# One quantising chain over 1536 values a step in the FFN tail of a graph transformer layer

## The chip, the cores and the metric

The kernel runs on one core of a Trainium2 chip. Its time is the device time of an execution in microseconds; the time shown for a kernel is the median of its runs. The engines meant below are TensorE (PE), VectorE (DVE), ScalarE (ACT), GpSimd (POOL) and SyncE (SP), each with its own queue of instructions that run in order and wait for semaphores.

## The reference

The layer adds to `x` (1250 rows of 1024) a graph attention over 40000 edges and a linear (softmax-free) attention, and then a feed-forward block whose three products run on values rounded to FP4 (NVFP4: 16 values share one FP8 scale). The feed-forward part, which the change touches:

```
def fake_quant_nvfp4(x, global_scale):
    xb = x.reshape(sh[:-1] + (sh[-1] // BLOCK, BLOCK))            # BLOCK = 16
    amax = jnp.max(jnp.abs(xb), axis=-1, keepdims=True)
    sc8 = jnp.clip(amax / FP4_MAX * global_scale, 0.0, FP8_MAX).astype(jnp.float8_e4m3fn)
    dq = sc8 / global_scale
    a = jnp.clip(jnp.abs(xb) / safe_dq, 0.0, FP4_MAX)
    q = jnp.sign(xb) * _FP4_VALS[jnp.digitize(a, _FP4_MIDS)]
    return (q * dq).reshape(sh)
gate_out = nvfp4_linear(x, gate_w, s_in[0])                      # x: layernormed rows, 1024 wide
up_out = nvfp4_linear(x, up_w, s_in[0])
hidden = jax.nn.silu(gate_out) * up_out                          # 512 wide
return nvfp4_linear(hidden, down_w, s_in_down[0])
```

## The kernel before

The 1250 rows are held as C = 10 chunks of 128. Most of the kernel (to about 720 us) gathers messages for the graph attention on GpSimd, VectorE and ScalarE while TensorE works through large fp32 products. The tail, from about 720 us to the end, is a software pipeline over the chunks, written out by hand for each engine as a loop over steps k. It is in these lines:

- VectorE (L1658 to L1674), step k: residual additions that are due (`residual`, L1592: PSUM product plus the stored row, with its sum); `tail_scales(k)`, which forms the gated product of chunk k-1 (L1558), the block maxima of its 512 values and of the 1024 normalised values of chunk k+1 (L1247), and from both together the FP8 scales and their inverses (`scales`, L1212 to L1222); `rows_rounded(k+1)`, the chain of eight instructions of `quantized` (L1236 to L1244) over the 1024 values, which ends with `q_done`; residuals due at (k, 1); `hidden_rounded(k-1)`, the same chain over the 512 values, which ends with `h_done`; residuals due at (k, 2). Every instruction of a chain waits for the one before through a semaphore (`step`), except the last.
- TensorE, step k: `turn_q(k+1)` (L922, transposes of the quantised rows, waits for `q_done`); x2 products due (L900 and L903, fp32; for chunks 6 to 9 and a half of 5 they include 16 products, a residual's bank must be free); `down(k-2)` (transposes L944, products L955); `gate_up(k+1)` (L933).
- ScalarE, step k: `turn_over(k+1)` (L1153, copies the transposed rows, `q_taken`); `normalize(k+2)` (L1018, L1019, `ln2_done`); the copy of the transposed products of chunk k-2 (L1180); silu of chunk k+1 (L1188) behind `gate_up(k+1)`; `scale_down(k-2)` (L1145); `deviation` of a chunk whose residuals are complete (L1130 to L1135), at places fixed by the plan.
- GpSimd takes the root for a deviation (L712) and adds the scaled products of a chunk to the stored output (L718); SyncE stores rows.

Which x2 product is made and added at which step is fixed in the table `X2_PLAN` (chunk, half, bank, made at, added at): (8,1) and (8,0) are made in steps 2 and 3, (9,1) in step 4 in the bank of (8,0), (9,0) in step 5 in the same bank. (8,0) is added at (4, 1), (9,1) at (5, 1) and (9,0) at (6, 1), which in the kernel before is between the two chains of a step. Products for chunks 0 to 9 of the feed-forward block run with steps -1 to 12.

`ln2` (normalised rows), `silu` and `hidden` are separate pieces of the memory `round_mem`; `ln2` and `silu` are doubled by parity, `hidden` is single.

Of the kernel before, what the change touches and what calls it, by code (L numbers as in the profile page):

```python
# [6 lines left out]
ALU = mybir.AluOpType  # L7
# [3 lines left out]
BF16 = mybir.dt.bfloat16  # L11
I32 = mybir.dt.int32
U8 = mybir.dt.uint8
U16 = mybir.dt.uint16
# [4 lines left out]
D = 1024  # L19
# [7 lines left out]
I = 512  # L27
C = 10
EARLY = 6
NC = 128  # L30
# [3 lines left out]
KB = D // P  # L34
# [14 lines left out]
FP4_MAX, FP8_MAX = 6.0, 448.0  # L49
QB = 16  # L50
SCALE = (D // 16) ** -0.5
EXPONENT = 0x7F800000
CELL, MIDDLE = 0xFFE0, 0x0010
BINADE, HALF_BIT = 0x7F80, 0x0040
# [62 lines left out]
def gps_layer(nc, x, src, dst, rms_w, w_down, wl, wr, att, w_up, wq, bq, wk_t, bk, wv_t, bv,  # L117
# [9 lines left out]
    with ExitStack() as ctx:  # L127
# [76 lines left out]
        cscale = sb("cscale", [P, 3])  # L204
# [10 lines left out]
        acc = ps("acc", [P, 4, HALF])  # L215
# [52 lines left out]
        tail_scaled = sem("tail_scaled")  # L268
# [11 lines left out]
        q_done, q_tp, q_taken = sem("q_done"), sem("q_tp"), sem("q_taken")  # L280
        gu_full, silu_done, hid_done = sem("gu_full"), sem("silu_done"), sem("hid_done")
        h_done, h_tp, h_taken = sem("h_done"), sem("h_tp"), sem("h_taken")
# [4 lines left out]
        bias_bc = base[:, C - 1, :]  # L287

        tail_mem = round_mem
        silu = [tail_mem[0:NC, i * I:(i + 1) * I] for i in range(2)]  # L290
        ln2 = [tail_mem[0:NC, (1 + i) * D:(2 + i) * D] for i in range(2)]
        qa = tail_mem[0:NC, 3 * D:4 * D]
        row_cells, row_steps = (qa[:, i * I:(i + 1) * I].bitcast(BF16) for i in range(2))
        hidden = tail_mem[0:NC, 4 * D:4 * D + I]
        q_bf = [tail_mem[0:NC, (9 + i) * I:(10 + i) * I].bitcast(BF16) for i in range(2)]
        q_t = [tail_mem[:, (11 + i) * I:(12 + i) * I].bitcast(BF16).rearrange("p (k n) -> p k n", k=KB) for i in range(2)]
        h_bf = [tail_mem[0:NC, 13 * I + i * 256:13 * I + (i + 1) * 256].bitcast(BF16) for i in range(2)]
        h_t = [tail_mem[:, 14 * I + i * 256:14 * I + (i + 1) * 256].bitcast(BF16).rearrange("p (k n) -> p k n", k=4)
               for i in range(2)]
        base_at = [xhat_t[:, :, c * NC:(c + 1) * NC] for c in range(C)]  # L300
        gnn_tr = xr_sb[:, :, :].rearrange("p c f -> p (c f)")[:, 0:2 * NP].rearrange("p (k n) -> p k n", k=2)

        NB = (D + I) // QB
        blocks_of = tail_mem[0:NC, 15 * I:15 * I + 8 * NB].rearrange("p (a b) -> p a b", a=8)
        squares = tail_mem[0:NC, 15 * I + 8 * NB:16 * I + 8 * NB].bitcast(BF16)
        tail_max, tail_g = blocks_of[:, 0], blocks_of[:, 1]
# [671 lines left out]
        begun, n = ROUND_0_AT, index_of["p", 0]  # L978
        for g, (_, _, slots, _, _) in enumerate(ROUNDS):
            while n < len(groups):  # L980
                kind, i, engine = groups[n]
# [23 lines left out]
        def _(act):  # L1005
# [164 lines left out]
            for k in range(-1, C + 2):  # L1170
                if 0 <= k + 1 < C:
                    turn_over(k + 1)
                if 2 <= k + 2 < C:
                    normalize(k + 2)
                c = k - 2
                if 0 <= c < C:
                    act.wait_ge(h_tp, c + 1)
                    if c >= 2:
                        act.wait_ge(down_full, c - 1)
                    nc.scalar.copy(h_t[c % 2][:, :, 0:NC], tpb[:, 1, 0:4 * P].rearrange("p (k n) -> p k n", k=4)[:, :, 0:NC]).then_inc(h_taken, 1)  # L1180
                for c in whole_at((k, 0)) if k >= 0 else []:
                    deviation(c)
                c = k + 1
                if 0 <= c < C:
                    act.wait_ge(gu_full, c + 1)
                    if c >= 2:
                        act.wait_ge(hid_done, c - 1)
                    nc.scalar.activation(silu[c % 2], acc[0:NC, 2, :], ACT.Silu, scale=cscale[0:NC, 0:1]).then_inc(silu_done, 1)  # L1188
                if 0 <= k - 2 < C - 1:
                    scale_down(k - 2)  # L1190
                for c in [*whole_at((k, 1)), *whole_at((k, 2))] if k >= 0 else []:
                    deviation(c)

        @block.vector
        def _(dve):
            steps = [0]

            def step(ins):

                steps[0] += 1  # L1200
                ins.then_inc(dve_step, 1)
                dve.wait_ge(dve_step, steps[0])
# [21 lines left out]
            def quantized(v, to, factors, cell, way, width):  # L1224


                sc8, inv = factors
                nb = width // QB
                rows_in = v.shape[1] // width

                def turned_blocks(a):
                    return a.rearrange("p (r i b) -> p r i b", r=rows_in, i=QB)

                high = v.bitcast(U16).rearrange("p (r b i t) -> p r i b t", r=rows_in, i=QB, t=2)[:, :, :, :, 1]
                by_block = v.rearrange("p (b i) -> p b i", i=QB)
                step(nc.vector.tensor_tensor(by_block, by_block, inv.unsqueeze(2).to_broadcast([v.shape[0], rows_in * nb, QB]), ALU.mult))  # L1236
                step(nc.vector.tensor_scalar(turned_blocks(cell.bitcast(U16)), high, CELL, MIDDLE, ALU.bitwise_and, ALU.bitwise_or))
                step(nc.vector.tensor_scalar(way.bitcast(U16), cell.bitcast(U16), BINADE, HALF_BIT, ALU.bitwise_and, ALU.bitwise_or))
                step(nc.vector.tensor_scalar(way, way, 1.5, 64.0, ALU.max, ALU.mult))
                step(nc.vector.tensor_tensor(cell, cell, way, ALU.add))  # L1240
                step(nc.vector.tensor_tensor(way, cell, way, ALU.subtract))
                step(nc.vector.tensor_scalar(way, way, -FP4_MAX, FP4_MAX, ALU.max, ALU.min))
                spread = sc8.rearrange("p (r b) -> p r b", r=rows_in).unsqueeze(2).to_broadcast([v.shape[0], rows_in, QB, nb])
                return nc.vector.tensor_tensor(turned_blocks(to), turned_blocks(way), spread, ALU.mult)  # L1244

            def block_max(to, v):
                return nc.vector.tensor_reduce(to, v.rearrange("p (b i) -> p b i", i=QB), AX.X, ALU.max,  # L1247
                                               apply_absolute_value=True)
# [299 lines left out]
            def tail_scales(k):  # L1548


                lo, hi = 0 if k + 1 < C else D // QB, NB if k - 1 >= 0 else D // QB
                if k == -1:
                    nc.vector.tensor_copy(tail_g[:, 0:D // QB], s_in_bc[0:NC, 0:1].to_broadcast([NC, D // QB]))
                    step(nc.vector.tensor_copy(tail_g[:, D // QB:], s_in_bc[0:NC, 1:2].to_broadcast([NC, I // QB])))
                if k - 1 >= 0:
                    c = k - 1
                    dve.wait_ge(silu_done, c + 1)
                    nc.vector.scalar_tensor_tensor(hidden, acc[0:NC, 3, :], cscale[0:NC, 1:2], silu[c % 2], ALU.mult, ALU.mult).then_inc(hid_done, 1)  # L1558
                    dve.wait_ge(hid_done, c + 1)
                    ins = block_max(tail_max[:, D // QB:], hidden)  # L1560
                if k + 1 < C:
                    dve.wait_ge(ln2_done, k + 2)
                    ins = block_max(tail_max[:, 0:D // QB], ln2[(k + 1) % 2])
                step(ins)
                sc8, inv = tail_factors[k % 2]
                scales(tail_max[:, lo:hi], tail_g[:, lo:hi], (sc8[:, lo:hi], inv[:, lo:hi]),
                       (blocks_of[:, 2, lo:hi], blocks_of[:, 3, lo:hi])).then_inc(tail_scaled, 1)

            def rows_rounded(c):
                dve.wait_ge(tail_scaled, c + 1)  # L1570
                if c >= 2:
                    dve.wait_ge(q_tp, c - 1)
                sc8, inv = tail_factors[(c - 1) % 2]
                quantized(ln2[c % 2], q_bf[c % 2], (sc8[:, 0:D // QB], inv[:, 0:D // QB]), row_cells, row_steps, D).then_inc(q_done, 1)

            def hidden_rounded(c):
                dve.wait_ge(tail_scaled, c + 3)
                if c >= 2:
                    dve.wait_ge(h_tp, c - 1)
                sc8, inv = tail_factors[(c + 1) % 2]  # L1580
                quantized(hidden, h_bf[c % 2], (sc8[:, D // QB:], inv[:, D // QB:]), row_cells[:, 0:I], row_steps[:, 0:I], I).then_inc(h_done, 1)

            def residual(c, h):

# [75 lines left out]
            for k in range(-1, C + 3):  # L1660
                for i in added_at((k, 0)):
                    residual(*i)
                if k <= C:
                    tail_scales(k)
                if 0 <= k + 1 < C:
                    rows_rounded(k + 1)
                for i in added_at((k, 1)):
                    residual(*i)
                if k - 3 == C - 1:
                    finish(k - 3)  # L1670
                if 0 <= k - 1 < C:
                    hidden_rounded(k - 1)
                for i in added_at((k, 2)):
                    residual(*i)  # L1674

# [24 lines left out]
```

## Time and profile before

| | |
|---|---|
| median of 3 runs | 917.87 us (916.38 to 919.6) |
| profiled execution | 920.16 us |
| its span | 918.4 us |
| PE busy | 856.0 us (93%) |
| DVE busy | 817.6 us (89%) |
| ACT busy | 549.5 us (60%) |
| POOL busy | 498.9 us (54%) |
| mean granted clock of TensorE | 0.968 |

The span is the time from the first to the last instruction of the profiled execution; what lies around it makes its own time. All positions below are microseconds from the span's start. In a timeline, the busy time of an instruction is printed behind its start; where an instruction does not wait for the one ahead of it, it can start before that one's printed end. A chain "of 1024" is one whose instructions work on 1024 values in each of 128 partitions.

### The profile page before, as it was taken

How to read it: one execution, taken by the hardware profiler on the slowest of the kernel's cores; microseconds unless marked ns; L12 is line 12 of the kernel's file. 1: busy time of each engine (PE TensorE's matmuls, PEld its weight loads, DVE VectorE, ACT ScalarE, POOL GpSimd, SP SyncE). 2: the span in 40 equal slices, each digit the busy share in tenths (PEclk: the TensorE clock that was granted, in tenths of full speed). 3: DMA queues.
4: the chain of work that ended last, by engine and by line, in shares of the span. 5: the costliest groups of instructions: out<-in, count | busy, mean ns of one | idle time of the engine just before them, and what ended most of it. 6: DMA issues, size and time to landing. Idle time of an engine off the chain costs nothing.

```text
span 918.4 us, 9530 instructions
## 1 busy us (share of the span) xinstructions
PE 856.0 (93%) x2734; PEld 417.5 (45%) x2734; DVE 817.6 (89%) x987; ACT 549.5 (60%) x1947; POOL 498.9 (54%) x528
## 2 busy tenths in 40 slices
PE   4999999999999999999999999997999699999665
PEld 3885455644444444444444444432444244444222
DVE  7989988779999999999999999999994277999994
ACT  3313123356767887779898988798995332353432
POOL 5200748578667777777777787877775200010011
PEclk9999999999999999999999999997999899999877
DMA  9322625563655333663345633349959911113125
GB/s 306 98 95 52 179 85 178 143 196 99 84 162 184 97 89 89 193 202 107 102 122 172 193 97 100 91 111 190 382 111 204 207 49 46 69 24 69 24 46 87
DMA packets 72403, 117.85 MB, mean 128 GB/s; under 512 B 29383, under 2 KB 42340, under 8 KB 72330
## 3 DMA queue, kind: packets, MB, share of 16 engines
q0 software_dynamic: 27520, 63.68, 30.2%
q1 hardware_dynamic: 44826, 53.52, 18.6%
q8 instruction: 22, 0.36, 0.2%
q14 instruction: 35, 0.29, 0.1%
HBM read 89.15 MB, written 17.17 MB: 116 GB/s over the span
## 4 chain that ended last, share of the span: by engine, by line
DVE 61%; PE 14%; issue 9%; POOL 8%; DMA 6%; ACT 1%; ACTq 0%; SPq 0%; POOLq 0%; DVEq 0%
DVE acc_sb L1487 12%; DVE turned L1479 11%; DVE z L1639 11%; DVE turned L1637 10%; PE acc L745 3%; POOL round_mem L550 3%; PE turned L900 2%; DMA round_mem<-msg_table,idx 2%; PE acc L933 2%; DMA acc_sb<-gnn_dram 2%; PE acc L900 2%; PE turned L955 1%; POOL round_mem L628 1%; POOL perm_dram L599 1%; POOL xr_sb L632 1%
## 5 line engine op out<-in xcount | busy, mean ns | idle before, releaser
L550 POOL DMA_INDIRECT round_mem<-msg_table,idx x352 | 345.5, 982 | 99.5 <-issue 80.0
L1122 ACT ACTIVATE round_mem<-round_mem,pz 128x65 f32<-128x65 f32 x1408 | 354.1, 398 | 7.0 <-DVE acc_sb L1487 3.0
L745 PE MATMUL acc<-wslot,big_a 128*128 128x512 f32 x512 | 220.3, 592 | 0.0
L745 PEld LDWEIGHTS acc<-wslot,big_a 128*128 128x128 f32 x512 | 97.1, 190 | 121.5 <-issue 121.3
L1487 DVE TENSOR_REDUCE acc_sb<-round_mem 128x260 f32<-128x1820 f32 (+1 forms) x62 | 121.6, 1962 | 7.2 <-ACT round_mem L1122 5.1
L1479 DVE TENSOR_TENSOR turned<-round_mem,turned 128x1560 f32<-128x1560 f32 (+1 forms) x62 | 105.4, 1700 | 7.4 <-DMA round_mem<-msg_table,idx 5.4
L1112 ACT ACTIVATE pz<-z 128x7 f32<-128x7 f32 (+1 forms) x248 | 55.4, 296 | 93.7 <-DVE z L1644 93.6
L745 PE MATMUL acc<-big_b,wslot 128*128 128x512 f32 x256 | 110.1, 592 | 0.2 <-ACT big_b L1058 0.2
L745 PE MATMUL acc<-wslot,big_b 128*128 128x512 f32 x256 | 110.0, 592 | 0.0
L1639 DVE TENSOR_REDUCE z<-turned 128x24 f32<-128x1560 f32 (+1 forms) x62 | 105.1, 1695 | 2.1
L1637 DVE SCALAR_TENSOR_TENSOR turned<-turned,att_sb 128x1536 f32<-128x1536 f32 (+1 forms) x62 | 103.6, 1671 | 0.0
L745 PE MATMUL acc<-big_a,xhat_t 128*128 128x512 f32 x192 | 84.8, 605 | 6.8 <-ACT big_a L1065 6.8
L745 PE MATMUL acc<-big_b 128*128 128x512 f32 (+3 forms) x240 | 80.6, 495 | 0.0
L745 PEld LDWEIGHTS acc<-big_b,wslot 128*128 128x128 f32 x256 | 48.6, 190 | 61.7 <-issue 60.5
L745 PEld LDWEIGHTS acc<-wslot,big_b 128*128 128x128 f32 x256 | 48.6, 190 | 61.2 <-issue 60.7
L712 POOL TENSOR_TENSOR rstd<-small,minus_half 128x1 f32<-128x1 f32 x10 | 6.3, 632 | 107.0 <-ACT small L1135 107.0
L745 PEld LDWEIGHTS acc<-big_a,xhat_t 128*128 128x128 f32 x192 | 37.2, 194 | 54.4 <-issue 46.8
L745 PEld LDWEIGHTS acc<-big_b 128*128 128x128 f32 x240 | 43.1, 194 | 35.3 <-issue 29.6
L667 POOL TENSOR_TENSOR round_mem<-acc_sb,pz 128x260 f32<-128x260 f32 x62 | 45.6, 736 | 21.8 <-DVE acc_sb L1487 21.0
L718 POOL DMA_DIRECT2D out_x<-acc_sb x9 | 8.0, 892 | 72.7 <-ACT acc_sb L1145 72.7
L1188 ACT ACTIVATE round_mem<-acc,cscale 128x512 f32<-128x512 f32 x10 | 6.9, 688 | 62.5 <-PE acc L933 62.5
L1055 ACT COPY big_a<-acc 128x512 f32<-128x512 f32 x16 | 9.2, 587 | 58.1 <-PE acc L745 42.6
(231 smaller groups left out, 1045.4 us busy)
## 6 DMA issues: line engine op xcount, KB each, us to landing
round_mem<-msg_table,idx POOLq DMA_INDIRECT x352, 2.8
big_b<-in_x SPq DMA_DIRECT2D x9, 512.0 KB, 7.7
big_b<-big_b SPq DMA_DIRECT2D x9, 512.0 KB, 13.2
big_b<-in_x POOLq DMA_DIRECT2D x9, 512.0 KB, 12.8
out_x<-big_b SPq DMA_DIRECT2D x9, 512.0 KB, 3.2
out_x<-acc_sb POOLq DMA_DIRECT2D x9, 512.0 KB, 5.4
wslot<-in_wv_t SPq DMA_DIRECT2D x2, 2048.0 KB, 9.3
wslot<-in_wk_t SPq DMA_DIRECT2D x2, 2048.0 KB, 9.5
```

The source lines that it names most:

```text
L550: pool.indirect_dma_start(xg[g % 4][:, j, :], None, msg_table, bass.IndirectOffsetOnAxis(idx[:, c, j0 + j:j0 + j + 1], 0)).then_inc(xg_in[ ...
L667: nc.gpsimd.tensor_tensor(halves_of[g % 3][:, :, :, n].rearrange("p i (h d) -> p i h d", d=MR), running[c].rearrange("p (i h d) -> p i h d ...
L745: mm = nc.tensor.matmul(o(acc[:, n % 4, :]), a, b, start=first, stop=last)
L900: nc.tensor.matmul(to, xhat_t[:, k, c * NC:(c + 1) * NC], mat_a[:, k, h * HALF:(h + 1) * HALF], start=(k == 0), stop=False)
L933: mm = nc.tensor.matmul(acc[0:NC, 2 + h, :], q_t[c % 2][:, k, 0:NC], wgu_sb[:, k, h * HALF:(h + 1) * HALF], start=(k == 0), stop=(k == KB ...
L1055: nc.scalar.copy(mat_a[:, m, h * HALF:(h + 1) * HALF], a).then_inc(t, 1)
L1112: ins = nc.scalar.activation(pz[:, g % 2, 0:slots + 1, h], z[:, g % 3, 0:slots + 1, h], ACT.Exp, scale=-1.0, bias=z[:, (g + 1) % 3, top_sl ...
L1122: ins = nc.scalar.activation(to[:, :, j], xg[g % 4][:, j, h * HR + 1:(h + 1) * HR], ACT.Copy, scale=pz[:, g % 2, j, h:h + 1])
L1479: return nc.vector.tensor_tensor(m4[:, 0:n], xg[g % 4][:, 0:n, :].rearrange("p j (h d) -> p j h d", d=HR)[:, :, :, 0:MR], receiver.unsquee ...
L1487: nc.vector.tensor_reduce(running[c].rearrange("p (i f) -> p i f", i=2), halves_of[g % 3][:, :, :, 0:n + 1], AX.X, ALU.add).then_inc(sum_d ...
L1637: step(nc.vector.scalar_tensor_tensor(m4[:, 0:slots, :, 1:MR], m4[:, 0:slots, :, 1:MR], 0.0, att_sb[0:NC].unsqueeze(1).to_broadcast([NC, s ...
L1639: step(nc.vector.tensor_reduce(zz[:, 0:slots, :], m4[:, 0:slots], AX.X, ALU.add))
```

## The change

The two chains of a step become one. The normalised rows of chunk k+1 and the gated products of chunk k-1 have the same parity, and stand side by side in a slab of 1536 values, two slabs by parity; the gated product is written over silu in place. One reduction takes the block maxima of both, and one chain of seven instructions runs over the 1536 values (1024 in steps -1 and 0, 512 in steps 9 and 10); its eighth, the multiplication by the scales, remains two instructions, first the one for the rows (`q_done`), then the one for the products (`h_done`). They read a part of each group of 96 block columns. Residuals that were due between the two chains come behind the fused one. ScalarE's silu waits for `h_done` in place of `hid_done`. The scratch pieces move within `round_mem`.

```diff
-        silu = [tail_mem[0:NC, i * I:(i + 1) * I] for i in range(2)]
-        ln2 = [tail_mem[0:NC, (1 + i) * D:(2 + i) * D] for i in range(2)]
...
-        hidden = tail_mem[0:NC, 4 * D:4 * D + I]
+        NB = (D + I) // QB
+        slab = [tail_mem[0:NC, i * (D + I):(i + 1) * (D + I)] for i in range(2)]
+        ln2, silu = [a[:, 0:D] for a in slab], [a[:, D:D + I] for a in slab]
+        row_cells, row_steps = (tail_mem[0:NC, 6 * I + 768 * i:6 * I + 768 * (i + 1)].bitcast(BF16) for i in range(2))
...
                     if c >= 2:
-                        act.wait_ge(hid_done, c - 1)
+                        act.wait_ge(h_done, c - 1)
...
-                    nc.vector.scalar_tensor_tensor(hidden, acc[0:NC, 3, :], cscale[0:NC, 1:2], silu[c % 2], ALU.mult, ALU.mult).then_inc(hid_done, 1)
+                    nc.vector.scalar_tensor_tensor(silu[c % 2], acc[0:NC, 3, :], cscale[0:NC, 1:2], silu[c % 2], ALU.mult, ALU.mult).then_inc(hid_done, 1)
                     dve.wait_ge(hid_done, c + 1)
-                    ins = block_max(tail_max[:, D // QB:], hidden)
                 if k + 1 < C:
                     dve.wait_ge(ln2_done, k + 2)
-                    ins = block_max(tail_max[:, 0:D // QB], ln2[(k + 1) % 2])
-                step(ins)
+                step(block_max(tail_max[:, lo:hi], slab[(k + 1) % 2][:, lo * QB:hi * QB]))
...
-            def rows_rounded(c):
...
-            def hidden_rounded(c):
...
+            def step_rounded(k):
+                lo, hi = 0 if k + 1 < C else D // QB, NB if k - 1 >= 0 else D // QB
+                n = hi - lo
+                dve.wait_ge(tail_scaled, k + 2)
+                if k >= 1 and k + 1 < C:
+                    dve.wait_ge(q_tp, k)
+                if k >= 3:
+                    dve.wait_ge(h_tp, k - 2)
+                sc8, inv = (f[:, lo:hi] for f in tail_factors[k % 2])
+                v = slab[(k + 1) % 2][:, lo * QB:hi * QB]
+                by_block = v.rearrange("p (b i) -> p b i", i=QB)
+                high = v.bitcast(U16).rearrange("p (b i t) -> p i b t", i=QB, t=2)[:, :, :, 1]
+                cell, way = row_cells[:, 0:n * QB], row_steps[:, 0:n * QB]
+                step(nc.vector.tensor_tensor(by_block, by_block, inv.unsqueeze(2).to_broadcast([NC, n, QB]), ALU.mult))
...
+                step(nc.vector.tensor_scalar(way, way, -FP4_MAX, FP4_MAX, ALU.max, ALU.min))
+                way = way.rearrange("p (i b) -> p i b", i=QB)
+                for there, to, b0, b1, done in ((k + 1 < C, q_bf, 0, D // QB, q_done), (k - 1 >= 0, h_bf, D // QB, NB, h_done)):
+                    if there:
+                        nc.vector.tensor_tensor(to[(k + 1) % 2].rearrange("p (i b) -> p i b", i=QB), way[:, :, b0 - lo:b1 - lo],
+                                                sc8[:, b0 - lo:b1 - lo].unsqueeze(1).to_broadcast([NC, QB, b1 - b0]), ALU.mult).then_inc(done, 1)
...
-                if 0 <= k + 1 < C:
-                    rows_rounded(k + 1)
+                if k <= C:
+                    step_rounded(k)
                 for i in added_at((k, 1)):
                     residual(*i)
...
-                if 0 <= k - 1 < C:
-                    hidden_rounded(k - 1)
```

## Rows read from the trace of the kernel before

**Rows 1.** Windows, 840 to 860: stretch, length, busy PE/PEld/DVE/ACT/POOL, PEclk, DMA share, GB/s
```profile
840.00:860.00 20.00, 17.24 (x75) 7.91 (x73) 18.93 (x40) 8.74 (x14) 1.54 (x3) 1.00 0.18 28
```

**Rows 2.** Timeline, VectorE, step 4: start, us, engine line op, shapes [idle before <-releaser]
```profile
815.67 1.22 DVE L1247 TENSOR_REDUCE round_mem<-round_mem 128x64 f32<-128x1024 f32 x1 [0.96 <-ACT round_mem L1019]
```

**Rows 3.** Timeline, VectorE, step 2: gated product, maxima, scales, start of the rows' chain
```profile
780.57 0.75 DVE L1558 SCALAR_TENSOR_TENSOR round_mem<-acc,cscale,round_mem 128x512 f32<-128x512 f32 x1
781.36 0.69 DVE L1247 TENSOR_REDUCE round_mem<-round_mem 128x32 f32<-128x512 f32 x1
782.91 1.22 DVE L1247 TENSOR_REDUCE round_mem<-round_mem 128x64 f32<-128x1024 f32 x1 [0.87 <-ACT round_mem L1019]
784.17 0.26 DVE L1212 SCALAR_TENSOR_TENSOR round_mem<-round_mem 128x96 f32<-128x96 f32 x1
...
787.11 1.23 DVE L1236 TENSOR_TENSOR round_mem<-round_mem 128x1024 f32<-128x1024 f32 x1
```

**Rows 4.** Timeline, all engines, step 7: from the rows' multiply to the next maxima
```profile
872.44 0.69 DVE L1244 TENSOR_TENSOR round_mem<-round_mem 128x1024 bf16<-128x1024 bf16 x1
...
873.18 0.62 PE L922 MATMUL turned<-identb,round_mem 128*128 128x128 bf16 x8 [3.02 <-DVE round_mem L1244]
...
873.84 1.01 ACT L1153 COPY round_mem<-turned 128x1024 bf16<-128x1024 bf16 x1
...
875.14 1.24 ACT L1019 ACTIVATE round_mem<-big_b,less_mean,rstd 128x1024 f32<-128x1024 f32 x1
...
877.41 0.69 DVE L1247 TENSOR_REDUCE round_mem<-round_mem 128x32 f32<-128x512 f32 x1
```

**Rows 5.** Timeline, VectorE: last multiplies of step 2's two chains, and of step 8's rows
```profile
792.27 0.69 DVE L1244 TENSOR_TENSOR round_mem<-round_mem 128x1024 bf16<-128x1024 bf16 x1
792.88 0.69 DVE L1236 TENSOR_TENSOR round_mem<-round_mem 128x512 f32<-128x512 f32 x1
...
796.13 0.42 DVE L1244 TENSOR_TENSOR round_mem<-round_mem 128x512 bf16<-128x512 bf16 x1
796.47 0.69 DVE L1592 SCALAR_TENSOR_TENSOR big_b<-acc,big_b 128x512 f32<-128x512 f32 x1
...
887.35 0.69 DVE L1244 TENSOR_TENSOR round_mem<-round_mem 128x1024 bf16<-128x1024 bf16 x1
```

**Rows 6.** Timeline, ScalarE: the copies L1153 of chunks 3 and 4, and what precedes
```profile
796.83 0.99 ACT L1153 COPY round_mem<-turned 128x1024 bf16<-128x1024 bf16 x1
...
809.55 0.69 ACT L1188 ACTIVATE round_mem<-acc,cscale 128x512 f32<-128x512 f32 x1 [3.42 <-PE acc L933]
810.14 1.11 ACT L1145 ACTIVATE acc_sb<-turned,cscale 128x1024 f32<-128x1024 f32 x1
...
813.18 0.99 ACT L1153 COPY round_mem<-turned 128x1024 bf16<-128x1024 bf16 x1
```

**Rows 7.** Timeline, TensorE, from the turning of q(3) to that of q(5)
```profile
794.01 0.61 PE L922 MATMUL turned<-identb,round_mem 128*128 128x128 bf16 x8
...
809.78 0.62 PE L922 MATMUL turned<-identb,round_mem 128*128 128x128 bf16 x8 [0.26 <-DVE round_mem L1244]
...
821.68 3.62 PE L933 MATMUL acc<-wslot,round_mem 128*128 128x512 bf16 x16
825.78 0.62 PE L922 MATMUL turned<-identb,round_mem 128*128 128x128 bf16 x8 [0.49 <-DVE round_mem L1244]
```

**Rows 8.** Timeline, VectorE: the last residual, with the feed-forward result of chunk 9
```profile
911.61 1.28 DVE L1597 SCALAR_TENSOR_TENSOR big_b<-turned,cscale,big_b 128x1024 f32<-128x1024 f32 x1 [5.45 <-PE turned L955]
```

**Rows 9.** Timeline, TensorE: down(1), and down(4) with gate_up(7) behind it
```profile
819.94 1.90 PE L955 MATMUL turned<-wslot,round_mem 128*128 128x512 bf16 x8 [0.68 <-ACT round_mem L1180]
...
862.40 3.59 PE L955 MATMUL turned<-wslot,round_mem 128*128 128x512 bf16 x8 [3.92 <-ACT round_mem L1180]
865.79 4.37 PE L933 MATMUL acc<-wslot,round_mem 128*128 128x512 bf16 x16
```

**Rows 10.** Windows, 862 to 864 (columns as in Rows 1)
```profile
862.00:864.00 2.00, 1.60 (x4) 0.58 (x5) 1.97 (x3) 0.35 (x1) 0.00 (x0) 0.50 0.97 180
```

More of the change, by code:

```diff
@@ L289, in gps_layer @@
         tail_mem = round_mem
-        silu = [tail_mem[0:NC, i * I:(i + 1) * I] for i in range(2)]
-        ln2 = [tail_mem[0:NC, (1 + i) * D:(2 + i) * D] for i in range(2)]
-        qa = tail_mem[0:NC, 3 * D:4 * D]
-        row_cells, row_steps = (qa[:, i * I:(i + 1) * I].bitcast(BF16) for i in range(2))
-        hidden = tail_mem[0:NC, 4 * D:4 * D + I]
+        NB = (D + I) // QB
+        slab = [tail_mem[0:NC, i * (D + I):(i + 1) * (D + I)] for i in range(2)]
+        ln2, silu = [a[:, 0:D] for a in slab], [a[:, D:D + I] for a in slab]
+        row_cells, row_steps = (tail_mem[0:NC, 6 * I + 768 * i:6 * I + 768 * (i + 1)].bitcast(BF16) for i in range(2))
         q_bf = [tail_mem[0:NC, (9 + i) * I:(10 + i) * I].bitcast(BF16) for i in range(2)]
-        q_t = [tail_mem[:, (11 + i) * I:(12 + i) * I].bitcast(BF16).rearrange("p (k n) -> p k n", k=KB) for i in range(2)]
-        h_bf = [tail_mem[0:NC, 13 * I + i * 256:13 * I + (i + 1) * 256].bitcast(BF16) for i in range(2)]
+        h_bf = [tail_mem[0:NC, 11 * I + i * 256:11 * I + (i + 1) * 256].bitcast(BF16) for i in range(2)]
+        q_t = [tail_mem[:, (12 + i) * I:(13 + i) * I].bitcast(BF16).rearrange("p (k n) -> p k n", k=KB) for i in range(2)]
         h_t = [tail_mem[:, 14 * I + i * 256:14 * I + (i + 1) * 256].bitcast(BF16).rearrange("p (k n) -> p k n", k=4)
@@ L301, in gps_layer @@
         gnn_tr = xr_sb[:, :, :].rearrange("p c f -> p (c f)")[:, 0:2 * NP].rearrange("p (k n) -> p k n", k=2)
-        NB = (D + I) // QB
         blocks_of = tail_mem[0:NC, 15 * I:15 * I + 8 * NB].rearrange("p (a b) -> p a b", a=8)
@@ L1567, in tail_scales @@
                        (blocks_of[:, 2, lo:hi], blocks_of[:, 3, lo:hi])).then_inc(tail_scaled, 1)
-            def rows_rounded(c):
[L1570 to L1574, printed above, removed]
-            def hidden_rounded(c):
[L1577 to L1581, printed above, removed]
+            def step_rounded(k):
[12 more added lines that the diff above has]
+                step(nc.vector.tensor_tensor(by_block, by_block, inv.unsqueeze(2).to_broadcast([NC, n, QB]), ALU.mult))
+                step(nc.vector.tensor_scalar(cell.bitcast(U16).rearrange("p (i b) -> p i b", i=QB), high, CELL, MIDDLE, ALU.bitwise_and, ALU.bitwise_or))
+                step(nc.vector.tensor_scalar(way.bitcast(U16), cell.bitcast(U16), BINADE, HALF_BIT, ALU.bitwise_and, ALU.bitwise_or))
+                step(nc.vector.tensor_scalar(way, way, 1.5, 64.0, ALU.max, ALU.mult))
+                step(nc.vector.tensor_tensor(cell, cell, way, ALU.add))
+                step(nc.vector.tensor_tensor(way, cell, way, ALU.subtract))
+                step(nc.vector.tensor_scalar(way, way, -FP4_MAX, FP4_MAX, ALU.max, ALU.min))
[4 more added lines that the diff above has]
+                                                sc8[:, b0 - lo:b1 - lo].unsqueeze(1).to_broadcast([NC, QB, b1 - b0]), ALU.mult).then_inc(done, 1)
```

## Prediction

> **What bounds the kernel now.** Only the FFN tail is touched, so I read the busy time of each engine by stretch first. In 840 to 860 us VectorE is busy 18.93 us of 20 and TensorE 17.24 [rows 1]: two engines close to full, so a saving on one is soon stopped by the other, and by whoever hands work between them. Then the timeline of VectorE: its last idle time before the end of the loop is 0.96 us ahead of the block maxima at 815.67, for the normalised rows from ScalarE [rows 2]; from there to the last multiply of step 8 at 887.35 it runs without a gap. Ahead of that, step 2 begins after TensorE's x2 product (its maxima wait 0.87 us for ScalarE too) [rows 3]. Last, the handover. Quantised rows q(k+1) leave VectorE; TensorE turns them; ScalarE copies them (L1153) and only behind that copy, in its own order, normalises chunk k+2 (L1018, L1019), which VectorE needs for the block maxima of step k+1. In step 7 this path reads: L1244 of 1024 values starts at 872.44 and ends at 873.13, the turning starts 873.18, the copy 873.84, L1019 875.14, ending 876.38 [rows 4]. That is 3.25 us from q done to the next normalised rows, 3.3 with the start of their user. Today VectorE works through the 512-value chain of the gated products meanwhile, and asks for the rows only with the second maxima instruction, about 878.0 (the first starts at 877.41 [rows 4] and takes 0.59 more when not waited for), so 1.6 us to spare.
>
> **The change, part by part.** Steps k = 1 to 8 have both halves; steps -1, 0 (rows only), 9 and 10 (products only) keep their work.
>
> (a) Seven elementwise instructions over 1536 replace seven of 1024 and seven of 512. Seven of 1024 take 792.27 - 787.11 = 5.16 us, seven of 512 take 796.13 - 792.88 = 3.25 [rows 3, 5]. On a straight line, 512 values cost 1.91 and the fixed part of seven is 1.34; the fused seven cost 5.16 + 1.91 = 7.07. The eighth stays two instructions: q's 0.61 (792.88 - 792.27), the products' 0.34 (796.47 - 796.13). Two chains were 9.36 us, the fused one is 8.02: 1.34 less VectorE time per step, 10.7 in eight steps.
>
> (b) One TENSOR_REDUCE over 1536 for two. 512 values take 0.69, 1024 take 1.26 start to start (784.17 - 782.91) [rows 3]; on the line 1536 take 1.83. The pair took 0.59 + 1.26 when nothing was waited for, so nothing is gained (0.02). But the 512-value maxima no longer run while VectorE waits for the normalised rows: in step 2 the maxima end 0.57 later.
>
> (c) q is done later in the chain. Before, it was done 5.16 + 0.69 = 5.85 us after the chain's start; now 7.07 + 0.69 = 7.76, 1.9 later. The products are done at 8.10 in place of 9.4 to 10.0; nobody is late for them now (they are turned a step later).
>
> (d) What VectorE has to do between q done and the next need of the normalised rows shrinks from 0.5 + 3.6 + 0.75 + 0.6 to the products' multiply (0.34, about 0.25 of it behind q's end), L1558 (0.78), and a residual or two (0.61 each) in steps 4 to 6. ScalarE's 3.3 us are then no longer covered: VectorE waits some 2 us in each step. That wait replaces the saving. Behind it on VectorE stand the maxima, the scales and the whole chain, and for its q TensorE and ScalarE.
>
> (e) silu(c) waits for h_done(c-2) instead of hid_done(c-2). It is signalled 0.35 us behind q_done(c), long before gate_up(c) can end: nothing; with that cover gone it would be 0.35 us. The writing of the products over silu's buffer and the new places in memory change no size: nothing (at most a fraction of L1558's 0.75 us [rows 3], either way, and in step order it would show in that row).
>
> (f) The last multiply now reads 64 of 96 columns per group. No row shows that pattern. Lower end: 0.69 as before. Upper end: the rate of the fp32 L1236, 1.26 against 0.69; 0.57 a step, eight times 4.6. I take the lower, because its second operand is read repeated already at the same speed. In the Trainium skill, VectorE: DVE Perf Modes, What auto-detection actually checks, the fast two-operand mode wants 16-bit tensors with step 1; the pattern keeps both, and by it (f) is zero.
>
> **The sum.** Follow q_done, since everything else hangs on it. The loop without other delay: 3.3 to normalised rows, 1.83 maxima, 2.94 scales (787.11 - 784.17 [rows 3]), 7.76 chain, less the rounding of both ends, 15.75 us per step.
> Start: step 2 still begins with TensorE's product, at L1558 780.57, and its maxima at 782.91 as the rows come. q_done(3) = 782.91 + 1.83 + 2.94 + 7.76 = 795.4; before it was 792.27 + 0.69 = 792.96. Shift +2.5.
> Then six loops to q_done(9), 94.5 us, plus what ScalarE adds, where it isn't free when q has been turned (0.70 after q_done):
> - q(3): turned at 796.1, but ScalarE is in a deviation until 796.83 [rows 6], not moved by the change: +0.7.
> - q(4): silu(3), scale_down(0) and a deviation (809.55 to 813.18 [rows 6]) stand ahead of the copy and hang on gate_up(3), which moves with the turning of q(3), from 794.01 to 795.5 [rows 7]: the copy at 814.65, while q(4) = 795.4 + 15.75 + 0.7 = 811.85 is turned at 812.55: +2.1.
> - q(6): TensorE needs 15.5 us from turning one q to being ready for the next (809.78 to 821.68 + 3.62 [rows 7]). q(5) = 829.7. x2 (9,1) waits for the residual of (8,0), which now stands behind the whole chain: +0.55. gate_up(5) ends about 845.7, silu and scale_down 1.8 later (0.2 + 0.59 + 1.0): 847.5, against q(6) = 845.4 turned at 846.2: +1.3.
> - q(5), q(7), q(8): ScalarE is free or within 0.1.
> q_done(9) = 795.4 + 94.5 + 4.1 = 894.0. Before, 887.35 + 0.69 = 888.04 [rows 5]. **+6.0 us.**
> From q_done(9) to the end nothing on the path changes: its turning, gate_up(9), silu(9), the last chains of 512, down and the last residual at 911.61, which VectorE awaits for 5.45 us [rows 8]. So the end moves by the same 6.0. The profiled execution took 920.16 with a span of 918.4 (1.76 around it): span 924.4, execution 926.2. The median shown, 917.87, is 2.3 below that execution; the same 6.0 on it gives **923.9**.
>
> **Rivals.**
> (1) The fixed cost comes back; faster. If VectorE is the bound in itself, four steps (4 to 7) give 1.34 each, 5.4, and step 3 another 1.3 if TensorE's gaps of 0.26 and 0.49 [rows 7] can close; q(9) inside step 8 comes 1.9 later; end 888.0 - 6.7 + 1.9, or -4.8: 913.1. For it: VectorE has no gap after 815.67. Against: it needs the normalised rows within 1.1 us of q done, and rows 4 show 3.3. It would hold only if ScalarE normalised before copying, which its order forbids. The Trainium skill, VectorE: DVE Perf Modes, The TRN2 errata, says an operation from SBUF pays a fixed extra latency per instruction and advises bigger tiles; the trace agrees that the part exists (1.34 for seven). By that rule alone this rival would be right.
> (2) A tie. ScalarE's three delays (4.1) don't add, for they close while TensorE and VectorE wait, and residuals fit the waiting: 2.5 + 6 x 15.75, less the 95.1 that the six take now (888.04 - 792.96), is +1.9: 919.8. For it: three of six loops are undisturbed. Against: each delay was placed by a row.
> (3) TensorE's clock falls earlier; slower still. Now it is at 1.00 in 840 to 860 [rows 1] and drops to 0.50 (1.2 GHz) in 862 to 864 [rows 10], behind 3.92 us without work; the eight products there took 3.59 in place of 1.90 and the sixteen behind them 4.37 in place of 3.62 [rows 7, 9], 2.4 more together. The forecast gives gaps of 1 to 2.4 us ahead of q(4), q(5) and q(7). If one in the x2 part (the widest is ahead of q(5), 827.3 to 829.7) lowers it, and it comes back as there, that is 2.4 more: 926.3, twice 928.7. Against: gaps of 2 us stand in no full-clock part before 857, so the trace hardly says.
> (4) It doesn't do what it says, because the strided multiply is slow (f): q later by 0.57 in six loops and in step 2, 4.0 more: 927.9.
>
> **How the numbers follow.** Forecast +6.0 (4 to 7.5): 0.66. Rival 1: 0.10. Rival 2: 0.12. Rival 3: 0.08. Rival 4: 0.04. Time 923.9. Range: down to 920.5, which leaves out rival 1 and most of rival 2; up to 927.5, which takes in one fall of the clock. A measurement here can tell about 0.3%, 2.8 us. Faster 0.10, same 0.14 (rival 2 and the weakest form of the forecast), slower 0.76.
>
> **What would show it.** Right: VectorE busy some 11 us less in the tail, with an idle time of about 2 us ahead of L1247 in steps 3 to 8, ended by ScalarE's L1019; seven instructions of 1536 values whose sum is 7.07; TensorE waiting for L1244's successor 1 to 2.4 us ahead of q(4), q(5), q(7) and over 4 us ahead of q(8), q(9); the end 30.4 us behind q_done(9). Wrong: no wait ahead of L1247 (rival 1); the q multiply over 1 us (rival 4); x2 products of 512 columns at twice their time (rival 3); intervals between the q's below 15.7.

## The result and the profile after

The changed kernel takes 930.15 us (median of 4 runs, 928.43 to 931.02) against 918.15 us for the kernel before (median of 4 runs, with one more than in the table ahead of the prediction): ratio 1.0135, 95% interval 1.0114 to 1.0157. It is 12.0 us slower. The prediction said slower by 6.0, 923.9 us, range 920.5 to 927.5: the sign was right, half of the loss was missing, and the time lies outside the range. Its profiled execution took 930.23 us, with a span of 928.5.

The line of busy time of the changed kernel's page, then VectorE's table of waits from 755 us on: who waited, for whom, us in total, times, longest.

```profile
PE 857.4 (92%) x2724; PEld 417.7 (45%) x2734; DVE 807.3 (87%) x923; ACT 549.8 (59%) x1947; POOL 499.8 (54%) x528
```

```profile
DVE round_mem L1245 <- ACT round_mem L1017: 13.5, 8, 3.4
DVE round_mem L1580 <- PE turned L942: 9.5, 4, 3.9
DVE big_b L1602 <- PE acc L901: 5.5, 1, 5.5
DVE round_mem L1556 <- ACT round_mem L1186: 3.4, 1, 3.4
```

VectorE does 10.3 us less work than before (807.3 against 817.6), as the change intends. But where the table of before, from 755 us on, had 1.8 us of waits for the normalised rows, there are now 13.5, and a second wait of 9.5 us that the prediction doesn't name: the first instruction of the fused chain (L1580) waits for TensorE's turning of gated products (L942). TensorE signals this turning with the semaphore `h_tp`; VectorE may write a chunk's quantised products into their buffer only when those of two chunks earlier have been turned out of it. `q_tp` does the same for the rows. The chain itself, in the changed kernel's VectorE timeline of step 1 (answers rows 3 and rows 5 of before):

```profile
764.57 1.76 DVE L1580 TENSOR_TENSOR round_mem<-round_mem 128x1536 f32<-128x1536 f32 x1
766.37 1.46 DVE L1581 TENSOR_SCALAR round_mem<-round_mem 128x1536 uint16<-128x1536 uint16 x1
767.86 0.56 DVE L1582 TENSOR_SCALAR round_mem<-round_mem 128x1536 uint16<-128x1536 uint16 x1
...
771.04 0.56 DVE L1586 TENSOR_SCALAR round_mem<-round_mem 128x1536 bf16<-128x1536 bf16 x1
771.63 1.03 DVE L1590 TENSOR_TENSOR round_mem<-round_mem 128x1024 bf16<-128x1024 bf16 x2
772.58 0.68 DVE L1602 SCALAR_TENSOR_TENSOR big_b<-acc,big_b 128x512 f32<-128x512 f32 x1
```

Seven instructions of 1536 take 771.63 - 764.57 = 7.06 us, the two multiplies 0.95. (The row `x2` joins the multiplies of the rows and of the products.) That is the time of the two multiplies before, 0.61 and 0.34: the strided reads cost nothing.

The two waits of step 4, in the same timeline: first for the normalised rows, then, with the scales done at 820.74, for the turned products.

```profile
816.05 1.75 DVE L1245 TENSOR_REDUCE round_mem<-round_mem 128x96 f32<-128x1536 f32 x1 [3.36 <-ACT round_mem L1017]
...
820.48 0.26 DVE L1220 SCALAR_TENSOR_TENSOR round_mem<-round_mem 128x96 f32<-128x96 f32 x1
823.07 1.76 DVE L1580 TENSOR_TENSOR round_mem<-round_mem 128x1536 f32<-128x1536 f32 x1 [2.33 <-PE turned L942]
```

TensorE's timeline of the changed kernel around the same time (answers rows 7): it idles 1.92 us ahead of the turning of q(4) and of q(5), and the sixteen x2 products behind the first gap take 8.78 us, those behind the second 7.13. The second fence is the window 812 to 816, within the 8.78 us: the granted clock, 0.57 (the figure ahead of the DMA share 0.70), is mostly at its lower level of 1.2 GHz. Behind the second gap, from 831 to 835, it is 1.00.

```profile
811.75 0.62 PE L920 MATMUL turned<-identb,round_mem 128*128 128x128 bf16 x8 [1.92 <-DVE round_mem L1590]
812.21 8.78 PE L898 MATMUL acc<-big_a,xhat_t 128*128 128x512 f32 x16
820.82 1.88 PE L901 MATMUL acc<-wslot,xr_sb 128*128 128x512 f32 x4
822.54 0.39 PE L942 MATMUL turned<-identb,round_mem 128*128 128x128 bf16 x4
...
830.88 0.62 PE L920 MATMUL turned<-identb,round_mem 128*128 128x128 bf16 x8 [1.92 <-DVE round_mem L1590]
831.82 7.13 PE L898 MATMUL acc<-big_a,xhat_t 128*128 128x512 f32 x16 [0.32 <-DVE big_b L1602]
```

```profile
812.00:816.00 4.00, 4.00 (x12) 1.80 (x10) 0.69 (x2) 3.87 (x6) 1.44 (x2) 0.57 0.70 98
```

The tail of every profiled kernel can be laid out as three stretches: from the gated product of step 1 to q(3) done, from q(3) to q(9) done, and the last leg from there to the end of the span. The middle one is six loops, those of steps 3 to 8; the experiments e1 to e10 follow below. A q is done 0.69 us after its multiply starts; in the kernel before that is L1244 with 1024 values, in the changed one L1590.

| kernel | to q(3) | six loops, q(3) to q(9) | last leg |
|---|---|---|---|
| before | 32.84 | 16.76 16.00 16.29 15.57 15.55 14.91 = 95.08 | 30.36 |
| before, again (e8) | 32.84 | 16.77 15.97 16.15 15.71 15.54 14.92 = 95.06 | 28.87 |
| changed | 35.35 | 17.43 19.13 17.96 19.65 15.78 16.22 = 106.17 | 28.07 |
| forecast | 35.3 | 16.45 17.85 15.75 17.05 15.75 15.75 = 98.6 | 30.4 |
| e1 | 35.33 | 16.43 17.83 15.77 17.04 15.75 16.18 = 99.00 | 30.10 |
| e2 | 33.72 | 17.89 16.34 16.69 15.33 16.53 15.49 = 98.27 | 29.02 |
| e3 | 33.72 | 17.88 19.13 17.96 19.65 14.12 13.90 = 102.64 | 27.34 |
| e4 | 32.83 | 16.77 15.99 16.29 15.74 15.53 14.91 = 95.23 | 27.00 |
| e5 | 35.33 | 17.42 17.43 17.96 17.97 15.76 16.18 = 102.72 | 26.52 |
| e6 | 33.72 | 15.34 15.15 14.73 15.39 15.34 13.50 = 89.45 | 28.06 |
| e7 | 31.86 | 16.76 14.92 16.17 15.58 15.53 14.93 = 93.89 | 26.55 |
| e9 | 33.71 | 17.55 19.13 17.97 19.66 14.11 13.50 = 101.92 | 27.36 |
| e10 (e6 again) | 33.72 | 15.33 15.15 14.73 15.39 15.34 13.50 = 89.44 | 28.09 |

Up to q(9) the changed kernel is 2.5 + 11.1 = 13.6 us longer than before. Its last leg happens to be 2.3 shorter and it reached the tail 1.2 earlier (758.91 against 760.12): 10.1, the difference of the spans. The kernel before's profiled execution lies 2.0 above its median, which makes the 12.0 of the medians.

### The profile page after: what moved, and what is told of

It is laid out like the page before. It is cut to its first block, busy times and chain, and to the rows that moved or that the text cites. A ratio compares the mean times of both kernels' runs of the same rounds, so it can differ in the third digit from the quotient of the medians.

```text
span 928.5 us, 9458 instructions
## 1 busy us (share of the span) xinstructions
PE 857.4 (92%) x2724; PEld 417.7 (45%) x2734; DVE 807.3 (87%) x923; ACT 549.8 (59%) x1947; POOL 499.8 (54%) x528
## 4 chain that ended last, share of the span: by engine, by line
DVE 59%; PE 16%; POOL 10%; issue 10%; DMA 3%; ACT 1%; ACTq 0%; POOLq 0%; DVEq 0%
DVE acc_sb L1485 11%; DVE z L1649 10%; DVE turned L1477 10%; DVE turned L1647 10%; POOL round_mem L548 4%; PE acc L898 4%; PE acc L743 3%; PE acc L901 2%; PE turned L898 2%; DVE round_mem L1580 1%; POOL round_mem L626 1%; POOL perm_dram L597 1%; POOL xr_sb L630 1%; DVE z L1654 1%; DVE big_b L1442 1%
```

## The experiments

Three theories follow from the table of waits. Theory A: the loss that was not forecast is the wait for `h_tp` in front of the chain. Before, it stood ahead of the products' chain, 5.8 us later in the step; only the last multiply writes what it protects. Theory B: the handover over ScalarE (the copy of the turned rows, and the normalisation L1017 behind it) is the whole cause. Theory C: TensorE's clock has a part of its own.

**e1_wait_late.** The changed kernel, both waits for TensorE directly ahead of the multiplies they protect:

```diff
-                if k >= 1 and k + 1 < C:
-                    dve.wait_ge(q_tp, k)
-                if k >= 3:
-                    dve.wait_ge(h_tp, k - 2)
...
                     if there:
+                        if done is q_done and k >= 1:
+                            dve.wait_ge(q_tp, k)
+                        if done is h_done and k >= 3:
+                            dve.wait_ge(h_tp, k - 2)
                         nc.vector.tensor_tensor(to[(k + 1) % 2] ...
```

> The changed kernel with its two waits for TensorE (q_tp, h_tp) moved from ahead of the fused chain to directly ahead of the two multiplies that write what they protect. Theory A (most of the loss beyond the forecast is the wait for h_tp in front of the chain, 1.06 + 2.33 + 2.22 + 3.92 = 9.5 us of idle time in steps 3 to 6, of which part only stands in for other waits, and the falls of TensorE's clock that it brings about): about the forecast's 924 us, between 922 and 926, ratio to the kernel before 1.004 to 1.009. Theory B (the handover over ScalarE, L1153 and L1017 behind it, is the whole cause, and the wait for h_tp only fills time that would be lost anyway): 928 to 930, unchanged.

Measured: 927.0 us beside 918.43 for the kernel before, 1.0084 (1.0064 to 1.0104). That is 3.2 us below the changed kernel, and 1 above the range that Theory A gave. In the table, though, e1 is the forecast almost to the digit: 99.0 for the six loops against 98.6, each loop within 0.02 of the sum but the last (16.18 against 15.75). There the turning of q(8) took 1.03 us in place of 0.62, at a granted clock of 0.50 from 879 to 880, and ScalarE's copy waits for it; that is 0.41 of the 0.43, a fall of the clock that the sum didn't have. TensorE's timeline, with the widest gap of the x2 steps, 2.32 us, above that turning:

```profile
830.32 0.62 PE L920 MATMUL turned<-identb,round_mem 128*128 128x128 bf16 x8 [2.32 <-DVE round_mem L1590]
831.26 7.13 PE L898 MATMUL acc<-big_a,xhat_t 128*128 128x512 f32 x16 [0.32 <-DVE big_b L1602]
...
878.88 1.03 PE L920 MATMUL turned<-identb,round_mem 128*128 128x128 bf16 x8 [5.22 <-DVE round_mem L1590]
```

VectorE's table of waits, from 755 us on, has no wait for L942 any more:

```profile
DVE round_mem L1245 <- ACT round_mem L1017: 15.5, 8, 4.4
DVE big_b L1607 <- PE turned L953: 5.7, 1, 5.7
DVE big_b L1602 <- PE acc L901: 5.5, 1, 5.5
DVE round_mem L1556 <- ACT round_mem L1186: 2.8, 2, 2.6
```

So the early waits cost 7.2 us between q(3) and q(9). e1 moves two of them, but only the one for L942 (`h_tp`) ever showed as idle time in the changed kernel. The spans differ by 3.4 only, for in its profiled execution e1 reached the tail 1.8 later (760.67 against 758.91) and had a last leg 2.0 longer. Theory B is right about the rest: 15.5 us of waits for ScalarE remain.

**e4_before_wait_early.** The kernel before, with the same wait also ahead of the rows' chain (the one ahead of the products' chain stays, and is then already met):

```diff
                 if c >= 2:
                     dve.wait_ge(q_tp, c - 1)
+                if c >= 4:
+                    dve.wait_ge(h_tp, c - 3)
                 sc8, inv = tail_factors[(c - 1) % 2]
```

> The kernel before with the wait for h_tp of a step moved ahead of the rows' chain (two chains kept). In it the turning of the products ends 0.4 to 0.7 us before the rows' chain starts in steps 3 to 5 and 0.03 after in step 6, so Theory A expects the same time within 0.2%: the early wait costs only together with the long chain. If moving the wait alone costs, 922 or more.

Measured: 917.9 beside 918.43, 0.9998 (0.9984 to 1.0011). The six loops take 95.23. The expectation of the same time held. The only trace of the wait in VectorE's table:

```profile
DVE round_mem L1236 <- PE turned L944: 0.2, 1, 0.2
```

The early wait is free with a chain of 5.85 us to q and dear with one of 7.76. It closes a loop: from the turning of q(k) over the x2 product and the turning of the products (9.5 us from start to end) to the start of the chain and on to q(k+1). With 0.2 us for the two handovers between the engines that loop went from 15.5 us, less than the 15.6 to 16.8 that steps 3 to 6 take before, to 17.4.

**e3_norm_first_only** and **e2_wait_late_norm_first.** ScalarE's order, with the changed kernel's waits (e3) and with e1's (e2):

```diff
+                if 2 <= k + 2 < C:
+                    normalize(k + 2)
                 if 0 <= k + 1 < C:
                     turn_over(k + 1)
-                if 2 <= k + 2 < C:
-                    normalize(k + 2)
```

> The changed kernel, waits as they are, with normalize(k + 2) ahead of turn_over(k + 1) on ScalarE. Theory A (the wait for h_tp bounds the x2 steps by itself: 9.5 us from the turning of q to that of the products, 7.8 us of chain, a period of 17.4): steps 3 to 6 keep their length, only 2, 7 and 8 gain, 923 to 927 us. Theory B (the handover over ScalarE is the cause): down to 915 to 919.

Measured, e3: 925.85, 1.0086 (1.0068 to 1.0104). Steps 3 to 6 keep their length to 0.5 us in the first and 0.01 in the others; 2, 7 and 8 gain 1.6, 1.7 and 2.3. That is Theory A's pattern, and the gain of 4.3 us its size.

> As e1, and on ScalarE normalize(k + 2) stands ahead of turn_over(k + 1), so that the next normalised rows don't wait for the turning of q. If both waits together are the cause of the loss, VectorE runs the fused chain without an idle time in steps 6 to 8 and TensorE bounds steps 2 to 5: q_done(9) about 885 in place of 888, 913 to 917 us, ratio 0.995 to 0.999. If the fused chain has a cost of its own (q being done 1.9 us later in the chain), 920 or more.

Measured, e2: 923.23, 1.0043 (1.0026 to 1.0059). Neither of the two expectations held as reasoned. The time is above 920, but not because the chain costs by itself: VectorE still waits for L1017, and e6 below, where it doesn't, is at 913.5.

```profile
DVE round_mem L1245 <- ACT round_mem L1017: 12.3, 6, 2.9
```

In e2's ScalarE timeline the normalisation is now late for what is left ahead of it: silu, `scale_down`, a deviation, and GpSimd's root for it.

```profile
810.03 0.69 ACT L1186 ACTIVATE round_mem<-acc,cscale 128x512 f32<-128x512 f32 x1 [3.42 <-PE acc L931]
810.62 1.11 ACT L1143 ACTIVATE acc_sb<-turned,cscale 128x1024 f32<-128x1024 f32 x1
811.61 0.20 ACT L1128 ACTIVATE mean_var<-mean_var 128x1 f32<-128x1 f32 x1
...
814.42 0.29 ACT L1016 ACTIVATE less_mean<-mean_var,rstd 128x1 f32<-128x1 f32 x1 [0.68 <-POOL rstd L710]
814.74 1.24 ACT L1017 ACTIVATE round_mem<-big_b,less_mean,rstd 128x1024 f32<-128x1024 f32 x1
```

**e5_clock_filled.** The changed kernel with 26 transposes whose results nobody uses, where TensorE idled:

```diff
-                pe.wait_ge(q_done, c + 1)
+                if not 4 <= c < 8:
+                    pe.wait_ge(q_done, c + 1)
                 if c >= 1:
                     pe.wait_ge(q_taken, c)
+                if 4 <= c < 8:
+                    pe.wait_ge(x2_taken, user_of(6))
+                    for j in range(26):
+                        nc.tensor.transpose(tpb[:, 0, 0:NC], wgu_sb[:, j % KB, 0:P], identb[0:NC, 0:NC])
+                    pe.wait_ge(q_done, c + 1)
```

> The changed kernel, waits as they are, with 26 idle transposes (weights into the bank of the turned rows, results unused) on TensorE ahead of the turning of q(4) to q(7), where it waited 1.92 us each time. Theory C (TensorE's clock, which fell behind two of these four gaps and made the sixteen x2 products take 8.8 us in place of 7.1, is a part of the loss of its own): all four take 7.1, q intervals of 17.4 to 18.0 in place of 19.1 and 19.7, 3.4 us less than the changed kernel, about 926.7. Theory A alone (the clock is hidden behind the waits): unchanged, 929 to 931.

Measured: 926.97, 1.0103 (1.0081 to 1.0126), 3.2 us below the changed kernel, though the two intervals overlap (that one is 1.0114 to 1.0157); the six loops are clearer: 102.72, 3.45 less. TensorE's timeline of e5:

```profile
811.07 1.61 PE L923 MATMUL turned<-identb,wslot 128*128 128x128 bf16 x26
813.14 0.62 PE L926 MATMUL turned<-identb,round_mem 128*128 128x128 bf16 x8 [0.46 <-DVE round_mem L1596]
813.60 7.09 PE L898 MATMUL acc<-big_a,xhat_t 128*128 128x512 f32 x16
```

All the x2 groups take 7.1 again, and the granted clock from 813.6 to 817.6 is 1.00. Theory C holds: two falls of the clock cost 1.7 us each, and work without any use wins them back.

**e6_fused_scalar_reordered.** e1, and on ScalarE the deviations that are due and then the normalisation of chunk k+3 ahead of the wait for `gate_up`; on GpSimd all roots of a step ahead of `add_to_stored` (not shown):

```diff
-                if 2 <= k + 2 < C:
-                    normalize(k + 2)
...
-                for c in whole_at((k, 0)) if k >= 0 else []:
+                for c in [*whole_at((k, 0)), *whole_at((k, 1)), *whole_at((k, 2))] if k >= 0 else []:
                     deviation(c)
+                if 2 <= k + 3 < C:
+                    normalize(k + 3)
...
-                for c in [*whole_at((k, 1)), *whole_at((k, 2))] if k >= 0 else []:
-                    deviation(c)
```

> The fused chain with late waits (as e1), and on ScalarE every deviation that is due and then normalize(k + 3) stand ahead of silu(k + 1), so that the normalised rows are ready a step early; GpSimd's roots stand ahead of its addition to the stored output. Theory A (fusing saves VectorE 1.34 us a step, and the loss is only in handovers): no idle time ahead of the block maxima, TensorE bounds steps 3 to 5 at 15.5, steps 6 to 8 take 13.5; q_done(9) about 882.5, 911 to 914 us. If q's later place in the chain costs by itself: 918 or more.

Measured: 913.54 beside 917.76, 0.9957 (0.9941 to 0.9974). The same kernel again, as e10:

> e6 once more, on the same chip as e9 for their comparison: 911 to 915 us, ratio to before 0.993 to 0.998.

Measured: 913.3 beside 919.03, 0.9934 (0.9911 to 0.9958), as expected. It is faster than both kernels; its two medians lie 0.4% and 0.7% below the kernel before. VectorE's waits in e6, from 750 us on, hold no L1017; of what is left, 6.1 us are for silu, that is, for TensorE:

```profile
DVE round_mem L1554 <- ACT round_mem L1186: 6.1, 4, 2.3
DVE big_b L1605 <- PE turned L953: 5.7, 1, 5.7
DVE big_b L1600 <- PE acc L901: 5.6, 1, 5.6
```

The expectation was met in the whole and in steps 3 to 5 (15.34, 15.15, 14.73), and missed in two of the last three: steps 6 and 7 wait 1.19 and 1.14 us for silu and take 15.39 and 15.34; only step 8 runs at 13.5.

**e7_before_scalar_reordered.** The kernel before with e6's order on ScalarE and GpSimd, two chains kept.

> The kernel before, two chains, with the same reordering of ScalarE and GpSimd. It had only 0.87 and 0.96 us of waits for normalised rows, and steps 6 to 8 are bound by VectorE at 14.9 to 15.5: Theory A expects 1 to 3 us less than before, 915 to 917, and 3 to 5 us more than e6. If the reordering is what brings e6's gain, both come to the same time.

Measured: 915.95 beside 917.76, 0.9982 (0.9968 to 0.9996). That is in the range given, but e6 is only 2.4 us below it, where 3 to 5 were expected. So 2.4 us is what fusing is worth once nothing waits for the handover. The table has the parts: 4.4 less in the six loops (93.89 to 89.45), and 1.9 more up to q(3) (31.86 to 33.72), for q comes later in the fused chain. The fixed parts of six steps would be 8.0. They don't come back whole because TensorE runs without a gap ahead of the turnings of q(4) to q(7) in e6, so that VectorE's saving is no gain there.

**e9_reordered_wait_early.** e6 with the two waits back ahead of the chain.

> As e6, but with the waits for TensorE ahead of the fused chain, as in the changed kernel. The wait for the turning of the products closes a loop of its own: from the turning of q(k) over 8.6 us of x2 product and the turning of the products (0.4) to the start of the chain, and 7.8 us of chain to q(k+1), 17.4 us. Theory A: steps 3 to 6 take 17.4 to 18 each in place of the 15.3, 15.2, 14.7 and 15.4 of e6 (some 9 us more), and where TensorE's clock falls behind the gap another 1.7 for each fall: 921 to 926 us. If the wait only filled other waits, as e6.

Measured: 923.52, 1.0063 (1.0042 to 1.0084), within Theory A's range, beside e10's 913.3 on the same chip: 10.2 us for the place of two waits. VectorE's waits from 755 us on:

```profile
DVE round_mem L1578 <- PE turned L942: 16.7, 4, 5.6
DVE big_b L1600 <- PE acc L901: 5.6, 1, 5.6
```

The loops of steps 3 to 6 are 17.55, 19.13, 17.97 and 19.66, to 0.15 those of the changed kernel, which had the ScalarE waits on top. In these four steps the early wait is therefore enough for the whole loss; behind it the handover over ScalarE is hidden.

**e8_before_again.** One more profile of the kernel before.

> The kernel before once more, unchanged, for the length of its last leg from q_done(9) to the end: 30.4 us in the profile of before, 27.0 in e4's, where the same instructions ran with TensorE at full clock in the last two down products. Expected: between 27 and 30.5, the steps between q(3) and q(9) within 0.3 us of the 95.1 of before.

Measured: 920.03, one execution. The loops agree with those of before to 0.02 us in their sum. The last legs of two executions of one program differ by 1.5 us, and e4's, with the same instructions, is 1.9 below that. In the last three down products of e4 TensorE runs at the speed of full clock, 1.90 us each; two of them, with the turning between:

```profile
901.39 1.90 PE L955 MATMUL turned<-wslot,round_mem 128*128 128x512 bf16 x8 [2.04 <-ACT round_mem L1180]
903.13 0.39 PE L944 MATMUL turned<-identb,round_mem 128*128 128x128 bf16 x4
904.97 1.90 PE L955 MATMUL turned<-wslot,round_mem 128*128 128x512 bf16 x8 [1.46 <-ACT round_mem L1180]
```

The same in the profile of before; these three rows are 2.5 us longer, of the 3.4 between the two legs:

```profile
900.25 2.46 PE L955 MATMUL turned<-wslot,round_mem 128*128 128x512 bf16 x8 [2.04 <-ACT round_mem L1180]
902.50 0.63 PE L944 MATMUL turned<-identb,round_mem 128*128 128x128 bf16 x4
904.39 3.60 PE L955 MATMUL turned<-wslot,round_mem 128*128 128x512 bf16 x8 [1.26 <-ACT round_mem L1180]
```

## Why the prediction was right and wrong

**The chain, (a) and (f).** Right: 7.06 us measured for 7.07 by the straight line; the multiplies keep their rate. Rival 4 falls.

**The maxima, (b).** 1.78 start to start against 1.83 (816.05 to the scales at 817.83). Right.

**q later, and the handover, (c) and (d).** Right. q(3) came 2.5 us late as summed, and VectorE waits 13.5 us for L1017, 1.1 to 3.4 in steps 3 to 8. ScalarE's three delays of 0.7, 2.1 and 1.3 stand in e1 where the rows of before put them. The terms of the undisturbed loop add up to 15.83, not 15.75, and the prediction gives no number for the rounding that it takes off; e1's two undisturbed loops are 15.77 and 15.75. So rival 2 falls, and so does rival 1. TensorE's gaps that the prediction named, 1 to 2.4 us ahead of q(4), q(5) and q(7) and over 4 ahead of q(8) and q(9), are 0.9, 2.3, 1.0, 5.2 and 4.8 in e1; in the changed kernel there are 1.9 ahead of each of q(4) to q(7).

**The step that failed: (e).** It took silu's new wait as the only one that moved, and called it free, which holds: every idle time of ScalarE ahead of a silu ends with `gate_up` in the changed kernel's timeline. The diff moves another: `h_tp` from ahead of the products' chain to ahead of the fused one. What was needed was at hand: the turning of q(4) begins at 809.78 [rows 7], and that of the products behind the x2 group ends at 819.27, 9.5 us later. Two rows of the kernel before, from the timeline of all engines:

```profile
818.88 0.39 PE L944 MATMUL turned<-identb,round_mem 128*128 128x128 bf16 x4
...
819.87 1.23 DVE L1236 TENSOR_TENSOR round_mem<-round_mem 128x1024 f32<-128x1024 f32 x1
```

A chain of 7.76 behind it makes 17.3, more than the 15.75 of the sum. The sum for the changed kernel should have taken the longer of two loops in steps 3 to 6. By e5, where the clock didn't fall in these steps, they take 17.4 in steps 3 and 4 and, as the x2 product there also waits for a residual, 18.0 in steps 5 and 6. An estimate with them is 2.5 + 102.3 - 95.1 = +9.7, or 927.6 on the median shown; the two falls of the clock, 3.4 more, would have made it 931.0, against 930.15 measured. e1 against the changed kernel gives 7.2 us of loops, e9 against e10 10.2 us in the medians. No idle time before could have shown this wait: the turning ended 0.6 us ahead of the rows' chain of that step (819.27 against 819.87), and the wait stood only ahead of the products' chain.

**The clock, rival 3.** Given 0.08, and it came, twice, at 1.7 us instead of 2.4. But it was not independent: it came with the gaps of 1.92 that the early wait made. e1, with one gap of 2.32 us in the same part, kept full clock (1.00 from 831 to 835); e2 with 2.27 did not (0.59 from 812.7 to 816.7).

**The transfer to the median.** The sum took the last leg as fixed at 30.4 and added 6.0 to the median. The leg is 27.0 to 30.4 in three executions of the same instructions, so a median difference of e1 (8.6) can differ from its difference up to q(9) (6.4). Whether e1's leg is typically longer than that of the kernel before, or its one profile was, stays open. The range had no term for it.

Up to q(9) the profiles account for 13.6 us: 6.4 are the handover and the later q of the forecast, 7.2 the early wait, 3.4 of these by way of the clock. The split goes by the order in which the causes are taken away: with ScalarE reordered first, the early wait is worth 12.5 in the six loops (e9 against e10), since each of the two waits hides a part of the other. Between that and the 12.0 of the medians stand the last leg and the start of the tail, which vary by more than the difference.

## What to carry to other kernels

When two chains become one, list each wait of both and ask where it now stands: a wait that protects one buffer belongs ahead of the instruction that writes it, not ahead of the chain, and moving it forward is free until the loop that it closes is the longest (here 15.5 us in steps of 15.6 to 16.8, then 17.4). Fusing saves the fixed parts but makes the first result later and removes the work that covered a handover; it paid only when the next input was made ready a step early. And a forecast for a software pipeline is the longest of all its loops per step, each summed, not the one followed first.

## What the runs showed of the hardware that was not expected

TensorE's granted clock fell behind gaps of about 2 us in the midst of otherwise full work. In the changed kernel it fell behind two of the three gaps of 1.92 us ahead of x2 products (0.57 from 812 to 816, 0.58 from 850 to 854, but 1.00 from 831 to 835). e3 and e9 slow down at the same two places, behind gaps of 2.26 and 1.91 in e3 and of 1.92 and 1.91 in e9, while e1's single gap of 2.32 us left the clock at full. So the length of the gap alone doesn't decide it, and no run here shows what does. After a fall the sixteen products took 8.8 us in place of 7.1. Filling 1.6 us of each gap with unused transposes kept all x2 products at 7.1, and the kernel became 3.2 us faster by doing more work.
